# A store that moves from GpSimd's queue to SyncE's, in a fused cross-attention and FFN block

## What is computed

```python
x = x + tanh(g_xattn) * xattn(layernorm(x), ctx, mask, wq, bq, wk, bk, wv, bv, wo, bo)
x = x + tanh(g_ffn)   * ffn(layernorm(x), w_gate, w_up, w_down, up_index, down_index)

def xattn(x, cond, mask, ...):              # 16 heads of 32
    q = int8_linear(x, wq, bq); k = cond @ wk.T + bk; v = cond @ wv.T + bv
    o = softmax(q @ k.T / sqrt(32) + mask) @ v
    return int8_linear(o, wo, bo)

def ffn(x, ...):                            # 512 -> 1408 -> 512
    g = fp8_linear(x, w_gate); u = fp8_linear(x, w_up)
    return fp8_linear(silu(g) * u, w_down)
```

## Time and profile before

| | |
|---|---|
| median of 3 runs | 570.88 us (569.48 to 573.16) |
| the profiled execution | 571.12 us, of which the span of the trace is 569.3 us |
| granted TensorE clock, mean over the span | 0.955 of full speed |
| busy: PE, DVE, ACT, POOL | 79%, 86%, 81%, 41% |
| instructions of DVE, ACT, POOL | 1254, 1129, 212 |
| chain that ended last, by engine | DVE 36%, POOL 14%, ACT 14%, issue 13%, PE 10%, DMA 5% |
| output stores by POOL | 7 from x2 and 1 from x_in, 512 KB each |
| DMA | 39.51 MB in the span, mean 69 GB/s |

### The profile page before, as it was taken

One profiled execution on the slowest core, in us unless ns is written; L12 is line 12 of the kernel. 1 busy time (PEld: TensorE's weight loads), 2 busy tenths in 40 slices (PEclk: granted clock), 3 DMA queues, 4 the chain that ended last, 5 costly groups with the idle time before them and its releaser, 6 DMA issues.

```text
span 569.3 us, 9874 instructions
## 1 busy us (share of the span) xinstructions
PE 449.5 (79%) x3030; PEld 272.7 (48%) x3030; DVE 487.7 (86%) x1254; ACT 461.4 (81%) x1129; POOL 232.8 (41%) x212
## 2 busy tenths in 40 slices
PE   0397496988998899889988988899889975963854
PEld 0274374555545554555455544554555443531321
DVE  5999789988798889888988798889888987699993
ACT  5779799998988798989888888898989886963350
POOL 4432262004653455246434642555246422541620
PEclk9999887999999999999999999999999998895967
DMA  8942352112114221322132113221321121000001
GB/s 259 387 139 79 98 149 56 38 57 38 56 27 94 62 57 26 89 68 57 27 104 52 57 26 84 74 55 27 91 65 20 27 53 30 20 0 16 20 17 74
DMA packets 61060, 39.51 MB, mean 69 GB/s; under 512 B 47568, under 2 KB 53712, under 8 KB 61008
## 3 DMA queue, kind: packets, MB, share of 16 engines
q1 hardware_dynamic: 56256, 27.47, 18.4%
q0 software_dynamic: 3328, 11.41, 6.3%
q10 hardware_dynamic: 1424, 0.01, 0.1%
HBM read 23.87 MB, written 4.19 MB: 49 GB/s over the span
## 4 chain that ended last, share of the span: by engine, by line
DVE 36%; POOL 14%; ACT 14%; issue 13%; PE 10%; DMA 5%; DVEq 0%; POOLq 0%; SPq 0%; ACTq 0%
POOL up L464 5%; POOL up L454 4%; DVE ts L1482 3%; ACT prob L655 3%; DVE q L1204 3%; POOL x L433 3%; DVE q_last L1305 3%; DVE prob L1305 2%; ACT q_last L655 2%; PE bank_h L887 2%; DVE rows L1421 2%; DVE t_sb L1199 2%; DVE stats L1411 2%; DMA t_sb<-in_L_ffn_w_up_dram,index 2%; ACT rows L571 2%
## 5 line engine op out<-in xcount | busy, mean ns | idle before, releaser
L454 POOL TENSOR_TENSOR up<-up,wgu_scale 128x512 f32<-128x512 f32 (+1 forms) x42 | 52.0, 1239 | 81.8 <-ACT up L635 81.8
L664 ACT ACTIVATE probT<-bank_h 128x512 f32<-128x512 f32 x128 | 68.5, 587 | 1.3 <-PE bank_h L887 0.7
L655 ACT ACTIVATE prob<-prob,neg_max 128x256 f32<-128x256 f32 x128 | 63.3, 498 | 5.5 <-DVE neg_max L1305 5.5
L655 ACT ACTIVATE q_last<-q_last,neg_max 128x256 f32<-128x256 f32 x128 | 63.5, 499 | 2.2 <-DVE neg_max L1305 2.1
L469 POOL TENSOR_TENSOR x<-x,y 128x512 f32<-128x512 f32 x14 | 19.9, 1423 | 101.6 <-DVE y L1495 101.6
L464 POOL TENSOR_TENSOR up<-gate,up 128x512 f32<-128x512 f32 (+1 forms) x42 | 59.5, 1423 | 3.7 <-DVE gate L1360 1.5
L1305 DVE CUSTOM_DVE_ANT_0 prob<-bank_h,mask_sb 128x256 f32<-128x256 f32 x128 | 47.4, 420 | 12.9 <-PE bank_h L828 12.9
L887 PE MATMUL bank_h<-ident,prob 128*128 128x128 f32 x256 | 39.9, 291 | 12.8 <-ACT prob L655 12.7
L1305 DVE CUSTOM_DVE_ANT_0 q_last<-bank_h,mask_sb 128x256 f32<-128x256 f32 x128 | 47.4, 417 | 0.0
L914 PE MATMUL bank_o<-probT,v_sb 128*32 128x256 f32 x512 | 36.0, 400 | 14.0 <-DVE v_sb L1233 8.0
L562 ACT ACTIVATE mag<-t_sb,ts 128x512 f32<-128x512 f32 (+1 forms) x42 | 28.6, 680 | 20.1 <-DVE ts L1487 12.6
(11 more groups left out here) (237 smaller groups left out, 1209.0 us busy)
## 6 DMA issues: line engine op xcount, KB each, us to landing
x_in<-in_x_dram SPq DMA_DIRECT2D x8, 512.0 KB, 3.6
c_in<-in_ctx_dram SPq DMA_DIRECT2D x8, 512.0 KB, 3.8
out_dram<-x POOLq DMA_DIRECT2D x7, 512.0 KB, 3.8
mask_sb<-in_mask_BxSxS_ff_dram SPq DMA_DIRECT2D x8, 256.0 KB, 3.0
t_sb<-in_L_ffn_w_down_dram SPq DMA_DIRECT2D x2, 704.0 KB, 5.5
t_sb<-in_L_ffn_w_down_dram POOLq DMA_DIRECT2D x2, 704.0 KB, 6.8
kf<-in_L_xattn_wq_dram SPq DMA_DIRECT2D x1, 1024.0 KB, 10.8
wkT<-in_L_xattn_wk_dram SPq DMA_DIRECT2D x1, 1024.0 KB, 13.5
```

The source lines that it names most:

```text
L454: pool.tensor_tensor(up[:, c % 2, 0:w], up[:, c % 2, 0:w], wu_scale[:, off:off + w], ALU.mult).then_inc(f["u_scaled"], 1)
L655: ins = act.activation(prob_of[slot4][:, t, :], prob_of[slot4][:, t, :], ACT.Exp, bias=neg_max[:, slot4, t:t + 1], scale=-1.0, accum_out=r ...
L664: act.activation(probT[:, (slot + 3) % 4, :, :].rearrange("p a b -> p (a b)"), HEAD_BANK[(slot + 3) % 4][:, :], ACT.Copy).then_inc(s["turn ...
```

## The change

The piece `out_store` is taken out of POOL's list and put into SP's. On SP it stands behind the two `o_turn` of the following step and ahead of `x_turn`, in steps 3 to 7 and, ahead of `x2_turn`, in the tail. It stores the same x2 and raises the same semaphore. The stores of the last two batches are issued at the very end of SP's list. All waits of POOL, `x2_add`'s wait for `stored` among them, stay as they were. Line numbers of pieces behind the insertion grow by 5 or 9 (`o_turn` 335 becomes 340, `x2_add` 433 becomes 442).

```diff
+                def out_store(slot):
+                    if b > 2:
+                        sp.wait_ge(s["out_ready"], 1 + 2 * (b - 2))
+                        sp.dma_start(out[bass.ds(b - 3, 1)].rearrange("o (t p) c -> p (o t) c", p=P), x2[:, :, :]).then_inc(s["stored"], 16)
...
             def steady_step_order(k):
-                k.o_turn(0); k.o_turn(1); k.x_turn(0); k.x_turn(1); k.x2_turn(0); k.x2_turn(1); k.x_load(0); k.t_turn(0)
+                k.o_turn(0); k.o_turn(1); k.out_store(0); k.x_turn(0); k.x_turn(1); k.x2_turn(0); k.x2_turn(1); k.x_load(0); k.t_turn(0)
...
             def tail_order(k):
-                k.o_turn(0); k.o_turn(1); k.x2_turn(0); k.x2_turn(1); k.t_turn(2); k.t_turn(0); k.t_turn(1); k.t_turn(3)
+                k.o_turn(0); k.o_turn(1); k.out_store(0); k.x2_turn(0); k.x2_turn(1); k.t_turn(2); k.t_turn(0); k.t_turn(1); k.t_turn(3)
...
             tail_order(blocks(NB))
 
+            sp.wait_ge(s["out_ready"], 1 + 2 * (NB - 1))
+            sp.dma_start(out[bass.ds(NB - 2, 1)].rearrange("o (t p) c -> p (o t) c", p=P), x2[:, :, :]).then_inc(s["stored"], 16)
+            sp.wait_ge(s_last["out_ready"], 1 + 2)
+            sp.dma_start(out[bass.ds(NB - 1, 1)].rearrange("o (t p) c -> p (o t) c", p=P), x_in[:, :, :]).then_inc(s["stored"], 16)
             sp.wait_ge(s["stored"], 16 * NB)
...
-                def out_store(slot):
-                    pool.wait_ge(f["out_ready"], 1 + 2 * (d - 1))
-                    pool.dma_start(out[bass.ds(b - 2, 1)].rearrange("o (t p) c -> p (o t) c", p=P), x2[:, :, :]).then_inc(s["stored"], 16)
...
-                k.gate_up(10); k.gate_up(11); k.out_add(13); k.out_add(15); k.out_store(16)
+                k.gate_up(10); k.gate_up(11); k.out_add(13); k.out_add(15)
...
-                k.out_add(13); k.out_add(15); k.out_store(16); e.out_store(16)
+                k.out_add(13); k.out_add(15)
```

More of the change, by code:

```diff
@@ L21 @@
 LEAD = 12
-SpBlocks = namedtuple('SpBlocks', """x_load ctx_load mask_load x_turn o_turn x2_turn t_turn""")
-PoolBlocks = namedtuple('PoolBlocks', """load x_var x2_add x2_var x_plus_bias up_scale gate_up out_add out_store""")
+SpBlocks = namedtuple('SpBlocks', """out_store x_load ctx_load mask_load x_turn o_turn x2_turn t_turn""")
+PoolBlocks = namedtuple('PoolBlocks', """load x_var x2_add x2_var x_plus_bias up_scale gate_up out_add""")
 ActBlocks = namedtuple('ActBlocks', """pro_round_q unit_mag_0 gate_tanhs pro_round_o wo_scaled oqT_high k_out_1 x_int o_int tT_high up_copy t_mag_0 t_mag_1
@@ L351, in t_turn @@
                         s[f"tT_low_{t}" if k < 2 else f"tT_high_{t}"], 16)
-                return SpBlocks(x_load, ctx_load, mask_load, x_turn, o_turn, x2_turn, t_turn)
+                return SpBlocks(out_store, x_load, ctx_load, mask_load, x_turn, o_turn, x2_turn, t_turn)
             def first_step_order(k):
@@ L469, in out_add @@
                     pool.tensor_tensor(x2[:, t, :], x2[:, t, :], y2[:, :], ALU.add).then_inc(f["out_ready"], 1)
-                def out_store(slot):
-                    pool.wait_ge(f["out_ready"], 1 + 2 * (d - 1))
-                    pool.dma_start(out[bass.ds(b - 2, 1)].rearrange("o (t p) c -> p (o t) c", p=P), x2[:, :, :]).then_inc(s["stored"], 16)
                 return PoolBlocks(
-                    load, x_var, x2_add, x2_var, x_plus_bias, up_scale, gate_up, out_add, out_store)
+                    load, x_var, x2_add, x2_var, x_plus_bias, up_scale, gate_up, out_add)
             def first_step_order(k):
```

## The result

The changed kernel takes 568.58 us (median of 9 runs, 566.31 to 569.45), the kernel before 571.03 us (9 runs, 569.48 to 573.16). The ratio is 0.9948, with a 95% interval of 0.9927 to 0.9968: 2.5 us less, less than 1%, but clear of the noise. I had forecast 570.4, a gain of 0.6 us. The gain is four times what I had added up.

A forecast was written before the change was run, and what follows sets the result against it. The prediction took the kernel as bound by a chain of dependent work through in-order engines, not bandwidth. Steps +0.4, exit -1.2, last landing +0.2 gave -0.6 from 571.12, so 570.5, stated as 570.4 us; range 568.3 to 575.0.

The forecast's parts named there:

- What bounds the kernel, and the rate: Dependent chain through in-order engines; at x2_add in each step, a microsecond of lateness is worth a microsecond of time.
- d: Time from the issue of SP's store to its landing, taken as 3.3 us.
- What is removed: POOL's issue of the store (0.79 us in step 5) and traffic beside the transposes go; counted nothing for steps 4 to 7.
- Step 3: x2_add's extra 1.14 us of lateness comes from the store beside the transpose and disappears; net -0.8 us with the new store.
- s: Start of the first transpose of the attention output (o_turn) in a step; times in the step count from it.
- Rival 2: In step 3 the lateness isn't the store's, so its 0.8 us gain stays away: 571.1 us; chance 13%.
- What is added: SP's store leaves 2.2 us later; x2_add at s + 6.0 at the earliest, 0.38 late in steps 4, 5, 7: +1.1 us.
- The end: After the last work: exit 1.2 us sooner because POOL's closing DRAIN waits for its own last DMA; last store's landing +0.2.
- The sum: All terms over the whole kernel: +0.4 - 1.2 + 0.2 = -0.6 us.
- Rival 1: At the steps' stores, d is 4.2 us or more: +5.6 us (1%) at 4.2; chance 9%, milder form 14%.
- Rival 3: At the kernel's end, POOL's closing DRAIN doesn't shrink: +0.6 for -0.6, 571.5 us; chance 10%.
- Rival 4: In all steps the path runs through the second transpose, 3.6 becoming 2.4 us: 8.3 us faster, 562.6; chance 4%.

The follow-up runs named there:

- the cut stores: Changed kernel with each store at a seam (between steps) cut into four of 128 columns: 575.90 us, ratio 1.0096 to the kernel before.

## Why the prediction was off

**What bounds the kernel, and the rate.** Right. Steps 3, 4, 6 and 7 last 50.4 to 50.6 us more than their x2_add is late, in every trace with the clock at full speed there and the store not between the transposes, for lateness from 5.6 to 7.6; in the two traces with half clock in step 3 it is 50.8 there. What was missing is the clock: I priced a late store at "7 us for each microsecond of d" as if that held anywhere. Two steps of the cut stores cost 2 to 3 us more; the tail, which I counted among the six, took no longer, but at a higher clock, so its price is open.

**What is removed.** Right that nothing comes of POOL's shorter list. In step 5 the two x_var operations began at 296.7 instead of 297.5 and the seam stayed where it was. Right, too, that the transposes land sooner without helping: the pair of step 4 took 2.4 us each.

**Step 3.** Right in its cause; the step that failed is the issue time in front of the new store. I said that the 1.14 us come from the store alongside and disappear, and they did: the first transpose landed in 3.1 us instead of 4.67 and y of tile 0 was ready 1.16 us sooner. But I put the new store at s + 2.6 in every step, after 2.50 us of issue. In step 3 SP took 3.24 us (of which 1.93 for the first of the pair), with no DMA of POOL near it, and the earlier trace rows already had 3.52 there. So the store landed at s + 6.3 and x2_add began at 6.34, not at 6.0: of the 0.76 that I had, 0.42 came in the first trace, and about 0.9 as an average over all traces. Rival 2 had a part of the size but not the reason: what stayed was the lateness of the new store.

**What is added.** The step that failed by size: d. I took 3.3, between the undisturbed store by POOL and the undisturbed load by SP; it was 3.0 (2.9 to 3.3). The bound from below, 3.1, was POOL's, and a store by SP is faster than that: 2.7 for 3.1 at the end of the kernel. I also read the earlier trace rows wrongly: the 3.3 of "3.3 to 4.1" is the store of batch 6 at 554 us, which had no transposes alongside; the six at the seams took 3.6 to 4.1. With d = 3.0 the store lands in front of y and steps 5, 6 and 7 cost nothing, where I had +0.8 for them. The Trainium skill's price in "DMA: Bandwidth & Descriptors", Anatomy of one DMA, an estimate of 3.2, was nearer than my 3.3 but is a fit to GpSimd's DMAs; the rows give 3.0 behind the transposes and 2.7 alone.

**The end.** The step that failed most: -1.2 + 0.2 = -1.0, and it was -2.0. The exit behind the landing was nearly right, 1.8 us before (569.3 - 567.5) and 0.4 after (566.8 - 566.4): -1.4 for my -1.2. The last store's landing has the wrong sign: I added d - 3.1 = +0.2 and it was 2.7 - 3.1 = -0.4, because I used a d that was meant for a store behind transposes where nothing stood ahead. And I left out the issue: SP's store starts 0.03 us behind the last addition, POOL's started 0.3 behind (564.36 against 564.06). That is -0.3 more. To two digits the three are -1.38, -0.37 and -0.27, together -2.0. The reason that I gave for the DRAIN, that it waits for POOL's own DMA, fits the three ends with a store on POOL, with a correction: without one it still runs on for 2.4 us behind POOL's last work.

**The sum.** With the sizes as the traces show them the seams are -0.1 in the first pair (-0.4 at step 3, +0.3 at step 4; -0.8 over all traces) and the end is -2.0, together -2.1 to -2.8, against -2.5 measured. The mechanisms were those that I had named; 1.0 of the missing 1.9 us lay in the size of the end, 0.5 to 1.2 in that of the seams. None of the rivals had a larger gain at the end, which is why the range stopped at 568.3.

**The rivals.** Rival 1, a long d, didn't come: nothing else was in flight, as I had said against it, and the cut stores show that it would indeed have turned the result (ratio 1.0096 with the last quarter 3.6 to 5.4 us behind the first issue). Rival 3 fell with the closing rows. Rival 4 fell as well: the second transpose landed sooner in all steps and the time did not follow.

## What to carry to other kernels

Price the last store of a kernel separately from the others: here nothing hid what followed the last computation, and one store out of eight, on another queue, took 2.0 us off the closing stretch, while the six at the seams gave less than can be measured. Look at the closing rows of the profile and ask which engine is the last to leave, and whether something is still waiting for a DMA of its own. And where a transfer gets a new place, check when its result is needed against the landing that its new queue gives alone, not against the landing that it had in company, and behind the issue times that its new queue has at each place. Where a wait has two conditions, compare both times with the start of the work: in step 3 the row named DVE, and the store had come later.

## What the runs showed of the hardware

- SP's store of 512 KB from SBUF landed 2.7 us after its issue at the end, 2.9 to 3.0 behind two transposes and, in one step, 3.3. In the kernel before POOL's took 3.1 and 3.3 with nothing alongside and 3.6 to 4.1 beside transposes. SP's issue took 0.37 to 0.58 us, POOL's 0.73 to 0.84.
- POOL's closing DRAIN ended 2.4 us behind its last computing instruction without a DMA, and 1.2 to 1.5 us behind the landing of its own last store, whether of 512 KB or of 32 KB. DVE's and ScalarE's DRAINs took 0.7 and 0.5 us.
- The granted clock fell to 1.2 GHz in step 3 after a wait of PE of 2.45 us in two traces and of 2.67 us in one, and stayed at 2.4 GHz in another after a wait of 2.72 us.
- Slow issues and slow landings on SP fall together with instruction loads at the places below. In the changed kernel the landing of 3.3 us, in step 4, has three of them alongside. DMA queues from 242.5 to 246 us (queue and kind: packets, MB, share of 16 engines):

```profile
q8 instruction: 1, 0.02, 2.1%
q14 instruction: 2, 0.02, 1.5%
```

  From 298.8 to 302 us, where the store took 3.0, there are none, and from 183 to 187 us, where the first transpose took 1.93 us to issue, there is one on q8. I did not test this; it is a coincidence seen at these places.
